# A state-space decoder block on one core: plain projection with diagonal taps, and u times B by ScalarE scaling and TensorE transposes for 4 of 16 state indices

## What is computed

```python
xz = x @ W_in.T;  x_ssm, z = jnp.split(xz, 2, axis=-1)
xc = conv_general_dilated(x_ssm transposed, conv_w, padding=[(3, 0)], feature_group_count=512)   # 4 taps for each channel
x_ssm = silu(xc + conv_b)
proj = x_ssm @ W_x.T;  B_ssm = proj[..., :16];  C_ssm = proj[..., 16:32]
dt = softplus(proj[..., -1:] * W_dt[:, 0] + b_dt);  A = -exp(A_log)
def step(h, inp):                       # over the 1024 tokens; h is 512 channels x 16 state indices
    dt_t, Bt, Ct, xt = inp
    h = exp(dt_t[..., None] * A) * h + (xt * dt_t)[..., None] * Bt[:, None, :]
    return h, einsum('bdn,bn->bd', h, Ct)
y = (ys + x_ssm * D_param) * silu(z)
x = layernorm(x + y @ W_out.T)
```

## Time and profile before

| | |
|---|---|
| median of 3 runs | 1843.66 us (1841.05 to 1845.77) |
| the profiled execution | 1843.35 us |
| its span, first to last instruction | 1841.6 us, so 1.75 us lie around it |
| state-space block, 16 turns | 54 to 998 us |
| attention and experts | 998 to 1841.6 us |
| busy over the span | PE 1483.1, DVE 1431.3, ACT 1110.4, POOL 919.3 us |

### The profile page before, as it was taken

The page is one execution under the profiler, slowest core; times in us unless marked ns, Lnnn a source line. Parts: engine busy times, 40 slices in busy tenths (PEclk is TensorE's granted clock), DMA queues, the critical chain, the costliest instruction groups (busy, mean ns, idle before and its releaser), DMA issues. The chain is left out here.

```text
span 1841.6 us, 23560 instructions
## 1 busy us (share of the span) xinstructions
PE 1483.1 (81%) x7984; PEld 1050.1 (57%) x7984; DVE 1431.3 (78%) x2667; ACT 1110.4 (60%) x2370; POOL 919.3 (50%) x758
## 2 busy tenths in 40 slices
PE   4777888777887888877866679988998899889880
PEld 3566667666776667765755345555545545464470
DVE  1899999999999999999997244395449654964578
ACT  2767877688667876787673224347634763376471
POOL 0687778877787778787785100004500460036005
PEclk9888899998898898889966879999999999999895
DMA  3311110111011110111010301000010001000000
GB/s 119 129 52 52 64 52 12 64 64 64 6 59 64 64 53 13 64 64 58 1 62 13 127 1 42 9 1 1 13 61 1 1 1 46 1 1 1 23 1 23
DMA packets 38331, 71.19 MB, mean 39 GB/s; under 512 B 3585, under 2 KB 31842, under 8 KB 33858
## 3 DMA queue, kind: packets, MB, share of 16 engines
q1 hardware_dynamic: 38210, 69.68, 11.1%
HBM read 61.02 MB, written 8.65 MB: 38 GB/s over the span
## 5 line engine op out<-in xcount | busy, mean ns | idle before, releaser
L635 POOL TENSOR_TENSOR state_c<-state,c_bc 128x1024 f32<-128x1024 f32 x256 | 601.5, 2361 | 127.1 <-DVE state L711 98.3
L711 DVE TENSOR_TENSOR_SCAN state<-decay,bu_ps 128x512 f32<-128x512 f32 x512 | 620.3, 1211 | 0.2 <-ACT decay L491 0.2
L491 ACT ACTIVATE decay<-dt_sb,negA 128x255 f32<-128x255 f32 x1024 | 432.4, 496 | 0.0
L686 DVE TENSOR_TENSOR bu_ps<-u_sb,b_ps 128x512 f32<-128x512 f32 x512 | 349.7, 683 | 50.6 <-POOL u_sb L556 37.4
L1330 POOL TENSOR_TENSOR big<-big,g_sb 128x1024 f32<-128x1024 f32 x29 | 79.2, 2733 | 619.0 <-ACT big L1215 617.7
L352 PE MATMUL y_ps<-ident_sb,state_c 128*128 128x128 f32 x2048 | 297.2, 293 | 18.1 <-POOL state_c L635 17.3
L352 PEld LDWEIGHTS y_ps<-ident_sb,state_c 128*128 128x128 f32 x2048 | 256.7, 152 | 53.3 <-POOL state_c L635 33.1
L273 PE MATMUL w_ps<-xT_sb,w_conv 128*128 128x256 f32 (+1 forms) x1024 | 237.1, 385 | 13.6 <-DVE w_conv L754 12.7
L273 PEld LDWEIGHTS w_ps<-xT_sb,w_conv 128*128 128x128 f32 x1024 | 193.1, 194 | 39.8 <-DVE w_conv L754 12.7
L336 PE MATMUL b_ps<-parts,sel_bc_sb 96*128 96x256 bf16 x256 | 75.7, 296 | 98.1 <-DVE bu_ps L702 74.9
L1398 DVE TENSOR_REDUCE neg<-ps 128x8 f32<-128x1232 f32 x64 | 91.0, 1436 | 69.7 <-PE ps L1009 69.7
(11 more groups left out here) (160 smaller groups left out, 2406.6 us busy)
## 6 DMA issues: line engine op xcount, KB each, us to landing
c_bc<-c_scratch SPq DMA_DIRECT2D x32, 1024.0 KB, 5.9
res<-in_x SPq DMA_DIRECT2D x16, 256.0 KB, 2.8
x_scratch<-res SPq DMA_DIRECT2D x16, 256.0 KB, 7.5
stage<-x_scratch SPq DMA_DIRECT2D x4, 1024.0 KB, 7.1
xa<-x_scratch SPq DMA_DIRECT2D x4, 1024.0 KB, 6.2
out_x<-acc SPq DMA_DIRECT2D x4, 1024.0 KB, 4.4
xT_sb<-in_xT SPq DMA_DIRECT2D x12, 259.0 KB, 3.4
w_sb<-in_w SPq DMA_DIRECT2D x2, 1024.0 KB, 12.7
```

Of the source, the lines that this page charges most:

```text
L491: nc.scalar.activation(decay[:, n % RING, j, 1:], dt_sb[:, i[1] % 2, j, 1:], ACT.Exp, scale=negA[:, j * NS + n:j * NS + n + 1]).then_inc(s ...
L635: nc.gpsimd.tensor_tensor(state_c[:, n % RING, :, :], state[:, n % RING, :, :], c_bc[:, q, n, :].unsqueeze(1).to_broadcast([P, CT, TC]), A ...
L686: nc.vector.tensor_tensor(bu_ps[m % 3][:, :].rearrange("p (j n) -> p j n", j=2), u_sb[:, i[1] % 2, 2 * h:2 * h + 2, :], b_ps[n % 2][:, 0:T ...
L711: nc.vector.tensor_tensor_scan(state[:, n % RING, pair, :].rearrange("p j n -> p (j n)"), decay[:, n % RING, pair, :].rearrange("p j n -> ...
```

## The change

The convolution is split. PE projects with the plain weights `w_ssm` (`in_proj`, 4 products for two channel tiles), ACT copies the result to SBUF as `xi` with the last 3 columns of the chunk before in front (`take_xi`), and PE convolves with four diagonal matrices for each channel tile (`conv`, 8 products for two tiles). The diagonals are built at the start by DVE in place of `w_conv`.

For the state indices 5, 8, 11 and 14 (`OFF`) DVE no longer multiplies u by B. PE transposes u once a turn (`turn_u`), ACT copies it (`take_u`), scales it for each of the four indices by the column of B for each token (`scale_u`, two instructions of 512 columns), and PE transposes it back (`fill`): the first half into the bank `b_ps` where the broadcast row stood, the second into `bu_ps`. B by token comes from two small transposes behind `step_row` (`take_bT`). The order of the work lists moves with it, `relu` now lies in `u_sb`, and the broadcast C has three half buffers, each load waiting for the products that used it.

The DVE makes 24 instead of 32 products a turn, all 32 scans stay. The heart of the diff:

```diff
+        OFF = (5, 8, 11, 14)
...
+            def in_proj(k, pair):
+                if pair == 0:
+                    pe.wait_ge(s_xT[q], loads(k))
+                    if not is_first(k):
+                        pe.wait_ge(s_uTc, at(k, CTT, 0))
+                else:
+                    pe.wait_ge(s_xic, at(k, 2, 1))
+                for e in range(2):
+                    j = 2 * pair + e
+                    for c in range(KT):
+                        last = nc.tensor.matmul(w_ps[:, e * TC:(e + 1) * TC], w_ssm[:, c, j * P:(j + 1) * P],
+                                                xT_sb[:, q, c, :], start=c == 0, stop=c == KT - 1)
+                last.then_inc(s_xi, 1)
+            def conv(k, pair):
+                if pair == 0:
+                    pe.wait_ge(s_xic, at(k, 2, 2))
...
+                else:
                     pe.wait_ge(s_xc, at(k, CT, 2))
...
+                for e in range(2):
+                    j = 2 * pair + e
+                    for back in range(TAPS):
+                        skip = back if first else 0
+                        last = nc.tensor.matmul(w_ps[:, e * TC + skip:(e + 1) * TC], diag_w[:, TAPS - 1 - back, j, :],
+                                                xi[:, j, HALO + skip - back:HALO + TC - back],
+                                                start=back == 0, stop=back == TAPS - 1, skip_group_check=True)
+            def fill(i, n, h):
+                if h == 0:
+                    b_free(i, n)
+                    pe.wait_ge(s_uB, CTT * (i[1] * K + OFF.index(n) + 1))
+                else:
+                    pe.wait_ge(s_scan, freed(i, n, 1))
+                dst, slot = place(i, n, h), (i[1] * K + OFF.index(n)) % 2
+                for e in range(2):
+                    for t in range(CTT):
+                        j = 2 * h + e
+                        last = nc.tensor.transpose(dst[:, e * TC + t * P:e * TC + (t + 1) * P],
+                                                   uB[:, slot, t, j * P:(j + 1) * P], ident_sb[:, :])
+                last.then_inc(s_fill, 1)
             def b_row(i, n):
+                if n in OFF:
+                    fill(i, n, 0)
+                    return
...
-                work = []
+                work = [(0, lambda: turn_u(i, 0)), (1, lambda: turn_u(i, 1))]
                 if prepare:
-                    work += [(0, lambda: conv(k, 0)), (1, lambda: conv(k, 1)), (3, lambda: conv(k, 2)),
-                             (4, lambda: conv(k, 3)), (5, lambda: z_tile(k, 0)), (6, lambda: z_tile(k, 1)),
-                             (8, lambda: project(k)), (9, lambda: step_row(k))]
+                    work += [(2, lambda: in_proj(k, 0)), (3, lambda: in_proj(k, 1)), (4, lambda: conv(k, 0)),
+                             (5, lambda: conv(k, 1)), (6, lambda: z_tile(k, 0)), (7, lambda: z_tile(k, 1)),
+                             (9, lambda: project(k)), (10, lambda: step_row(k))]
...
+                    if n + 1 in OFF:
+                        fill(i, n + 1, 1)
...
+            def scale_u(i, n):
...
+                for t in range(CTT):
+                    nc.scalar.activation(uB[:, o % 2, t, :], uT_sb[:, t, :], ACT.Copy,
+                                         scale=bT[:, i[1] % 2, t, n:n + 1]).then_inc(s_uB, 1)
...
+                work += [(3, lambda: take_u(i, 0)), (4, lambda: take_u(i, 1))]
                 if prepare:
...
+                    work += [(5, lambda: take_xi(k, 0)), (6, lambda: take_xi(k, 1)), (7, lambda: take_conv(k, 0)), (8, lambda: take_conv(k, 1)), (9, lambda: take_z(k, 0)),
+                             (10, lambda: take_z(k, 1)), (10, lambda: silus(k)), (12, lambda: copies(k)),
+                             (13, lambda: terms(k, 0)), (13, lambda: take_bT(k)), (13, lambda: terms(k, 1)),
+                             (13, lambda: terms(k, 2)), (13, lambda: terms(k, 3)), (13, lambda: softplus(k)),
                              (13, lambda: next_lead(k))]
+                work += [(n - 1, lambda n=n: scale_u(i, n)) for n in OFF]
...
             def make_bu(i, n, h):
+                if n in OFF:
+                    return
```

More of the change, by code:

```diff
@@ L62, in mamba_block @@
         SKIP_AT = 8
-        w_conv = sb("w_conv", [P, TAPS, KT, DI])
+        OFF = (5, 8, 11, 14)
+        K = len(OFF)
+        USES = [(n, h) for n in range(NS) for h in range(2) if n not in OFF or h == 1]
+        PROD = [(n, h) for n in range(NS) for h in range(2) if n not in OFF]
+        w_ssm = sb("w_ssm", [P, KT, DI])
+        diag_w = sb("diag_w", [P, TAPS, CT, P])
+        xi = sb("xi", [P, CT, HALO + TC])
         w_gate = sb("w_gate", [P, KT, DI])
@@ L189, in turns, with use, place, scanned @@
                 turn((None, r), prepare=r + 1 < NCH, finish=r >= 1, settle=r >= 2)
+        def use(i, n, h):
+            return i[1] * len(USES) + USES.index((n, h))
+        def place(i, n, h):
+            if n in OFF and h == 0:
+                return b_ps[n % 2]
+            return bu_ps[use(i, n, h) % 3]
+        def scanned(r, n, h):
+            return 2 * RING + r * 2 * NS + 2 * n + h + 1
+        def freed(i, n, h):
+            before = use(i, n, h) - 3
+            if before < 0:
+                return 0
+            return scanned(before // len(USES), *USES[before % len(USES)])
+        def multiplied(i, n, h):
+            return i[1] * len(PROD) + PROD.index((n, h)) + 1
+        def filled(i, n, h):
+            return 2 * (i[1] * K + OFF.index(n)) + h + 1
+        def broadcast(i, n):
+            return i[1] * (NS - K) + sum(m not in OFF for m in range(n + 1))
+        def added(i, n, h):
+            return (i[1] - i[1] // CPB - 1) * 2 * NS + 2 * n + h + 1
         block = ctx.enter_context(nc.Block())
@@ L258, in _ @@
         def _(pe):
-            def conv(k, j):
-                q, first = k[1] % 2, k[1] % CPB == 0
-                if j == 0:
+            def in_proj(k, pair):
+                q = k[1] % 2
+                if pair == 0:
                     pe.wait_ge(s_xT[q], loads(k))
                     if not is_first(k):
-                        pe.wait_ge(s_abs, at(k, 2 * CT, 0))
-                        pe.wait_ge(s_r, at(k, CTT, 0))
-                elif j == 2:
-                    pe.wait_ge(s_xc, at(k, CT, 2))
-                at_col = (j % 2) * TC
-                for back in range(TAPS):
-                    skip = back if first else 0
-                    for c in range(KT):
-                        last = nc.tensor.matmul(w_ps[:, at_col + skip:at_col + TC],
-                                                w_conv[:, TAPS - 1 - back, c, j * P:(j + 1) * P],
-                                                xT_sb[:, q, c, HALO + skip - back:HALO + TC - back],
-                                                start=back == 0 and c == 0, stop=back == TAPS - 1 and c == KT - 1,
-                                                skip_group_check=True)
-                if j % 2:
-                    last.then_inc(s_in, 1)
@@ L376, in turn @@
                         add_state(last, NS + n - LAG)
-                    for place, what in work:
-                        if place == n:
+                    if n + 1 in OFF:
+                        fill(i, n + 1, 1)
+                    for slot, what in work:
+                        if slot == n:
                             what()
             pe.sem_inc(s_r, 2 * CTT)
-            pe.wait_ge(s_wc, TAPS)
+            pe.wait_ge(s_in_w, 16)
             first = (None, 0)
-            for j in range(CT):
-                conv(first, j)
+            for pair in range(2):
+                in_proj(first, pair)
+            pe.wait_ge(s_wc, TAPS * CT)
+            for pair in range(2):
+                conv(first, pair)
             pe.wait_ge(s_gate_w, 16)
@@ L405, in _, with take_xi @@
         def _(act):
+            def take_xi(k, pair):
+                if pair == 0 and k[1]:
+                    act.wait_ge(s_in, at(k, 4, -2))
+                    if k[1] % CPB:
+                        nc.scalar.activation(xi[:, :, 0:HALO], xi[:, :, TC:TC + HALO], ACT.Copy).then_inc(s_halo, 1)
+                        act.wait_ge(s_halo, k[1] - k[1] // CPB)
+                act.wait_ge(s_xi, at(k, 2, pair + 1))
+                nc.scalar.activation(xi[:, 2 * pair:2 * pair + 2, HALO:HALO + TC],
+                                     w_ps[:, :].rearrange("p (j n) -> p j n", j=2), ACT.Copy).then_inc(s_xic, 1)
             def take_conv(k, h):
@@ L521, in _ @@
             first, last = (None, 0), (None, NCH - 1)
-            take_conv(first, 0)
-            take_conv(first, 1)
+            for pair in range(2):
+                take_xi(first, pair)
+            for pair in range(2):
+                take_conv(first, pair)
             for t in range(CTT):
```

185 lines of the change are left out of this document (122 added, 63 removed).

## The result

| | before | after |
|---|---|---|
| median | 1843.68 us (1841.05 to 1845.77, 4 runs) | 2002.87 us (1995.51 to 2007.69, 4 runs) |
| span of the profiled execution | 1841.6 us | 2005.9 us |
| busy over the span: DVE, ACT, PE | 1431.3, 1110.4, 1483.1 us | 1365.7, 1231.2, 1530.3 us |

The ratio is 1.086, with a 95% interval of 1.082 to 1.091: slower, as forecast (2004). DVE did lose the work that was to be taken from it, 65.6 us, and the kernel became 159 us longer. The four runs lie 12 us apart (1995.51 to 2007.69), and the profiled one, 2007.69, is the longest of them, so what is read from its trace stands up to 5 us above the median.

A forecast was written before the change was run, and what follows sets the result against it. It took the block as DVE-bound before (59.3 us a turn) and bound by a hand-over chain over w_ps after (71.2): 1841.6 + 155 + 16 - 5 - 5 = 2002.6, with 1.75 around the span 2004 us; range 1920 to 2060.

The forecast's parts named there:

- DVE's saving: State-space block: 8 products fewer a turn, 4.7 us, 75 us in all without stalls; nothing for scans following scans.
- ACT's work: ACT per turn: takes 1.9 us, eight scalings at 0.6 us 4.8; from 44.5 to some 51.5 of 53.8 us.
- The chain to index 11: From the variance over w_ps, silus and scalings: copies out at 28.8 us, index 11's second half 8.5 us late at full clock.
- The clock: PE at half rate after stands: 3.0 us a turn behind index 11's stand, 1.5 before in_proj(1).
- The 1.5 us before in_proj(1): PE waits 2.4 us for DVE, then 2.9 for ACT; up to 3 us of half rate, 1.5 taken.
- The sum: Whole kernel: 13 turns 155 us, first two turns 16, last turn -5, start -5, on 1841.6: 2002.6.
- DVE as the bound: Rival for the block: index 11 is ready when DVE wants it, 75 us and some 5 at the start go: 1763 us, chance 0.07.
- The chain at full clock: Rival for the block: same chain without half rate, turns of 66.7 us: 1937 us, chance 0.23 for 1850 to 1945.

The follow-up runs named there:

- the late guess: Against the changed kernel, ACT's guess of the old tile's rstd moved from step 5 to step 6, behind both takes of xi: 1983.4 us.
- PE kept busy: Against the changed kernel, 44 identity transposes into the shared bank, never read, between the last gate tile and the transposes for index 11: 1962.0 us.
- the early order: Against the split projection with no index offloaded (1913.5 us), its work on the shared bank starts at step 0 instead of two steps later: 1828.5 us.

## Why the prediction held, point by point

The turn whose rows stand above has DVE's step 3 at 550.40 us (its product there; t = 0). Further rows of it, from the timelines of DVE, ACT and POOL:

```profile
550.40 0.68 DVE L835 TENSOR_TENSOR bu_ps<-u_sb,b_ps 128x512 f32<-128x512 f32 x1
...
554.62 0.20 ACT L620 ACTIVATE lnv<-var 128x2 f32<-128x2 f32 x1 [6.66 <-POOL var L750]
...
596.21 2.35 POOL L698 TENSOR_TENSOR dt_sb<-dt_sb,u_sb 128x1024 f32<-128x1024 f32 x1 [3.84 <-ACT dt_sb L599]
...
604.14 0.17 DVE L856 TENSOR_TENSOR bu_ps<-bu_ps,inject 128x2 f32<-128x2 f32 x1 [2.71 <-PE bu_ps L400]
...
621.54 0.67 DVE L835 TENSOR_TENSOR bu_ps<-u_sb,b_ps 128x512 f32<-128x512 f32 x1
```

Against the predicted times:

| point | predicted | seen |
|---|---|---|
| variance read | 4.2 | 4.2 (554.62) |
| in_proj(1) out | 6.9 | 7.0 (557.42) |
| last gate tile out | 22.5 | 22.7 (573.10) |
| PE stands before index 11 | 5.3 long | 5.75 |
| copies for index 11 out | 28.8 | 29.6 (PE starts at 580.00) |
| start of index 11 to its second half's end, with the clock | 6.3 + 3.0 | 9.25 |
| second half of index 11 | 38.1 | 38.9 (589.25) |
| POOL starts make_dt | 44.9 | 45.8 (596.21) |
| second half of index 14, DVE's carry | 52.0 | 53.7 (604.14) |
| the turn | 71.2 | 71.1 (step 3 to step 3, to 621.54) |

From index 11 on, the predicted times above have the 3.0 us of the clock in them; the turn has the 1.5 us before in_proj(1) as well.

**DVE's saving.** Right in its premise: a scan behind a scan starts 1.13 to 1.14 us after it, as a product did, and a carry takes 0.05 to 0.13 us. Of busy time 65.6 us went, not 75. DVE has some 100 gaps more, and a scan is 1.21 us long where the next start follows after 1.13, so the 0.08 us of overlap is lost at each gap: about 8 of the missing 10 us, by this estimate.

**ACT's work.** The scaled copy had no row; 0.6 us was taken between 0.42 and 0.96, and the pair takes 1.24 us, so 0.62.

**The chain to index 11.** Each piece up to the gate tiles within 0.3 us in all, 0.8 late by the copies: the hand-overs between engines are 0.1 to 0.3 us each. What decided was forecast at the right place. One wait was missed: add_state of index 0 stands 2.0 us for DVE's product by the gate, and in_proj(0) follows it. So the chain has two heads that come almost together, which is why the late guess gave 1.6 us and not the 5 or more of a chain with one head.

**The clock.** 3.0 us at index 11 is right to 0.1 where the rate stays down, and 2.5 over all turns (69.2 to 66.7 with PE kept busy). The 1.5 us before in_proj(1) was wrong: PE stood 1.16 us for ACT there, not 2.9, and in_proj(1) ran at full rate. It had stood 2.28 and 2.02 us for DVE just before, and add_state of index 0 (1.97 us where the others take 1.04) and in_proj(0) (2.60 for 1.99) ran at half rate in part; but ACT was waiting for the variance meanwhile, so none of that reached the chain. In its place come the 0.8 us above and 0.7 more up to index 14: its transposes run at half rate behind a stand of 2.76 us, and so, in part, does add_state(11), 1.61 us, which is on the chain. So the right total contains a term too much and one too little. The rule of the Trainium skill ("TensorE: Matmul & The Clock Gate", HAM oscillation), half rate after each recurring stall, fits the stand of 5.75 us, which half rate followed in all 15 turns; behind the stand of 1.16 us none did. At index 11 the clock could be kept up with work that nobody reads.

**The sum.** 13 regular turns gave 11.5 us each (11.9 predicted, 155 against 150). The first two were 12.1 and 10.0, where 8 each was taken: without a variance they still wait for index 11. The last gave back 5.3 (5), the start 6.9 (5). Behind the block, where nothing was changed, 4.4 us more: from the last product by the gate to the end it is 839.5 us before and 843.9 after, and 837.1 with PE kept busy, so this differs from kernel to kernel; its cause is open. Against the forecast these are -5, +6, 0, -2 and +4 us, and they cancel to +3. That the forecast lies within 2 us of the median is luck to that extent, and the more so as the kernel's own runs lie 12 us apart.

**The rivals.** DVE as the bound would have been 75 us of gain; it comes to be the bound only with the projection early and no index offloaded. The Trainium skill ("Perfetto Trace Analysis", Identifying the Most-Contended Engine) would have had DVE relieved first, and every run that relieved it lost. The chain at full clock was put at 1937 us; the run with PE kept busy took 1962, with the clock kept up at index 11 alone: the transposes of index 14 still ran at half rate there (1.09 us for four).

**What the prediction did not see** is where the loss comes from. It made one chain with one deciding place, index 11. Taken apart, 5.1 us a turn come with the split projection alone: 5.7 for the two steps that it is late, since turn_u has taken the first two places on w_ps, less the 0.6 that it gains in the early order. Another 5.1 are the late indices 11 and 14 with their clock. Offloading 5 and 8 adds 0.1 us a turn and 9 us in all to the first, and gains nothing.

## What to carry to other kernels

Where engines hand one buffer round, write down the turn as times from one fixed point and ask of each added step what stands behind it on its in-order engine; the busy sums say whether the result can be good, the chain says whether it is. An added piece of work costs by its place: the same two copies moved up one step gave 73 us at one index and took 33 at another. Before a price is read from one turn of a trace, look at the same line over all turns.

## What the runs showed of the hardware

- The same stand of 5.75 us of TensorE, 15 times, was followed by half rate that cost 1.4 us in three turns and up to 3.0 in the others. What tells them apart was not found.
- 44 transposes that nobody reads (4.97 us) held the granted clock at 1.00 and made the kernel 2% faster (2002.87 to 1962.03 us).
- Two scans of 128x512 from PSUM one behind the other took 1.2 us each, 1.14 from start to start, as they did with a product between.
- ScalarE's copy of 128x512 with a scale per partition, within SBUF, took 0.62 us.
